# Second norm's root, inverse, shift and rows ahead of the score decays in each attention step, and the shared expert's weights split 512 columns at a time

## The reference, cut to what matters

```python
x = L0_attn_x
...
h = _layernorm(x, axis=-1) * (1 + ca) + sa
x = x + ga * _L0_attn_ref(h, slope_rate, W_qkvu, W_out)
h = _layernorm(x, axis=-1) * (1 + cb) + sb          # the second norm
x = x + gb * _L0_ffn_ref(h, wg, sh_gate, sh_up, sh_down, ex_gate, ex_up, ex_down)

def _layernorm(x, axis=-1, eps=1e-05):
    m = jnp.mean(x, axis=axis, keepdims=True)
    v = jnp.var(x, axis=axis, keepdims=True)
    return (x - m) / jnp.sqrt(v + eps)

# shared expert, over all tokens: silu(h @ sh_gate.T) * (h @ sh_up.T) @ sh_down.T
```

## Time and profile before

| what | us |
|---|---|
| median of 3 runs (lowest, highest) | 378.85 (378.01, 379.61) |
| the profiled execution, as timed | 375.64 |
| its span in the profile | 373.8 |
| attention steps 3 to 16 on TensorE | from 69.12 to 142.21 |
| feed-forward part | from 142.21 on |
| TensorE, VectorE, ScalarE, GpSimd busy, share of the span | 97%, 75%, 58%, 54% |

### The profile page before, as it was taken

The page is one execution under the profiler, slowest core; times in us unless marked ns, Lnnn a source line. Parts: engine busy times, 40 slices in busy tenths (PEclk is TensorE's granted clock), DMA queues, the critical chain, the costliest instruction groups (busy, mean ns, idle before and its releaser), DMA issues.

```text
span 373.8 us, 12932 instructions
## 1 busy us (share of the span) xinstructions
PE 362.9 (97%) x4978; PEld 315.0 (84%) x4983; DVE 280.2 (75%) x561; ACT 218.6 (58%) x453; POOL 200.8 (54%) x193
## 2 busy tenths in 40 slices
PE   8989998999999989999999999999999999999996
PEld 4546555778888769899999999999999999999995
DVE  7996388999899985579976987777777675555543
ACT  5688667677677755648276746555555634333222
POOL 2000003978778785311364687868767787674240
PEclk9999999999999999999999999999999999999999
DMA  8956031000197007999425465574685865665443
GB/s 265 375 63 60 2 134 37 2 4 30 32 353 184 31 31 265 330 336 271 88 92 108 104 110 104 95 118 88 104 109 91 100 101 103 100 114 77 70 58 113
DMA packets 53043, 45.35 MB, mean 121 GB/s; under 512 B 31524, under 2 KB 46996, under 8 KB 52856
## 3 DMA queue, kind: packets, MB, share of 16 engines
q1 hardware_dynamic: 43048, 32.09, 32.5%
q0 software_dynamic: 7488, 10.27, 18.2%
q10 hardware_dynamic: 2448, 2.18, 1.8%
HBM read 27.60 MB, written 10.49 MB: 102 GB/s over the span
## 4 chain that ended last, share of the span: by engine, by line
PE 72%; POOL 13%; DVE 7%; issue 5%; ACT 3%; ACTq 0%; POOLq 0%; DVEq 0%
PE ps L1630 37%; PE ps L1648 18%; PE ps L1413 7%; POOL tmp L554 3%; POOL tmp L558 2%; POOL tmp L575 2%; PE ps L1399 2%; POOL h2s L579 2%; POOL tmp L573 2%; POOL wx L563 2%; PE ps L1341 2%; DVE st L937 1%; PE ps L1533 1%; PE ps L1361 1%; DVE tmp L1254 1%
## 5 line engine op out<-in xcount | busy, mean ns | idle before, releaser
L1630 PE MATMUL ps<-tmp,wx 128*128 128x128 bf16 x1776 | 105.5, 219 | 0.0
L1630 PEld LDWEIGHTS ps<-tmp,wx 128*128 (+1 forms) x1776 | 102.3, 98 | 0.9 <-issue 0.2
L611 POOL DMA_INDIRECT out<-tmp,dk x39 | 72.0, 1846 | 38.0 <-SPq L515 32.5
L857 ACT ACTIVATE tmp<-tmp 128x512 bf16<-128x512 f32 x55 | 34.6, 629 | 80.8 <-PE ps L1648 61.6
L1648 PE MATMUL ps<-wx,tmp 128*128 (+1 forms) x660 | 80.7, 273 | 0.2 <-DVE tmp L1260 0.2
L1648 PEld LDWEIGHTS ps<-wx,tmp 128*128 128x128 bf16 x660 | 62.2, 98 | 6.9 <-DVE tmp L1260 0.5
L1254 DVE TENSOR_TENSOR tmp<-ps,tmp 128x512 f32<-128x512 f32 x55 | 37.9, 689 | 37.7 <-PE ps L1630 32.1
L1630 PE MATMUL ps<-w_hl,wx 128*128 128x128 bf16 x864 | 51.3, 219 | 0.9 <-ACT tmp L846 0.9
L606 POOL DMA_INDIRECT tmp<-h2rows,src_i x39 | 42.1, 1081 | 16.7 <-issue 10.8
L1630 PEld LDWEIGHTS ps<-w_hl,wx 128*128 (+1 forms) x864 | 49.6, 98 | 1.4 <-issue 1.0
L1260 DVE TENSOR_TENSOR tmp<-tmp 128x512 bf16<-128x512 f32 x55 | 38.3, 696 | 10.1 <-ACT tmp L857 9.9
(11 more groups left out here) (194 smaller groups left out, 555.2 us busy)
## 6 DMA issues: line engine op xcount, KB each, us to landing
wx<-in_wexp SPq DMA_DIRECT2D x26, 512.0 KB, 5.4
xres<-in_x SPq DMA_DIRECT2D x4, 512.0 KB, 6.6
h2rows<-h2s ACTq DMA_DIRECT2D x16, 128.0 KB, 3.4
out<-h2s SPq DMA_DIRECT2D x12, 128.0 KB, 2.1
h2s<-in_wmod SPq DMA_DIRECT2D x1, 1024.0 KB, 9.5
wx<-decay_rows SPq DMA_DIRECT2D x16, 64.0 KB
modr<-mod_rows SPq DMA_DIRECT2D x1, 1024.0 KB, 4.4
wx<-in_wqkvu SPq DMA_DIRECT2D x1, 768.0 KB, 6.8
```

The costliest lines, as they stand in the source:

```text
L611: e.indirect_dma_start(t["out"], bass.IndirectOffsetOnAxis(ap=dst_i[:, j:j + 1], axis=0), yb[(NA + j) % 2], None, compute_op=ALU.add).then ...
L857: e.activation(hs[p][:, 0:FF], hf[p], ACT.Copy).then_inc(s["inner_high"], 1)
L1630: ins = e.matmul(half(bank, m * P), weight(at_, weights(part, w) + k * FF + m * P, P), xT[f % NXT][:, (2 * a + k) * P:(2 * a + k + 1) * P] ...
```

## The change

VectorE: the decayed keys (L1075) now come behind the second norm's statistics (L1090). Behind them stand the inverse and the shift of the second norm (L1114 and L1116 before, L1098 and L1100 now), which stood behind the gated output; so they are ahead of the decay of the scores. ScalarE: the root (L746) comes ahead of the state's decay, and the normed rows (L774 before, L767 now) ahead of the squares and the turned rows. For the last tile (m = 15) VectorE makes the normed rows itself (L1105), and ScalarE at that place takes the silu of one column into a spare tile (L763). The shared weights are split in eight parts of 512 columns in steps 2, 3, 9, 10, 11, 12, 13, 14, where there were four of 1024 in steps 2, 9, 11, 13; the semaphore values that count parts are adapted.

```diff
-PARTS_AT, SCALED_AT = (2, 9, 11, 13), (0, 1, 2, 3)
+PARTS_AT, SCALED_AT = (2, 3, 9, 10, 11, 12, 13, 14), (0, 1, 2, 3)
...
@@ ScalarE, step_attention
                 if n and mine(n + 1):
                     mask_queries(n + 1)
+                if mine(m):
+                    wait(e, "ln2_moments", m + 1)
+                    e.activation(rs2[:, m % 2, 2:3], mv2[:, m % 2, 1:2], ACT.Sqrt, bias=epst[:, 0:1]).then_inc(s["ln2_root"], 1)
                 if mine(n, NSTATE) and n >= B:
...
-                if mine(m):
-                    wait(e, "ln2_moments", m + 1)
-                    e.activation(rs2[:, m % 2, 2:3], mv2[:, m % 2, 1:2], ACT.Sqrt, bias=epst[:, 0:1]).then_inc(s["ln2_root"], 1)
...
+                if m == NT - 1:
+
+                    e.activation(silu_back[:], epst[:, 0:1], ACT.Silu)
+                elif mine(m):
+                    wait(e, "ln2_shift", m + 1)
+                    wait(e, "h2_made", m - 1)
+                    e.activation(xn2[:, m % 2], xres[:, tile_of(m)[0]], ACT.Identity,
+                                 scale=rs2[:, m % 2, 3:4], bias=rs2[:, m % 2, 4:5]).then_inc(s["ln2_rows"], 1)
                 if mine(v):
                     wait(e, "values_added", v + 1)
...
-                if mine(m):
-                    wait(e, "ln2_shift", m + 1)
-                    wait(e, "h2_made", m - 1)
-                    e.activation(xn2[:, m % 2], xres[:, tile_of(m)[0]], ACT.Identity,
-                                 scale=rs2[:, m % 2, 3:4], bias=rs2[:, m % 2, 4:5]).then_inc(s["ln2_rows"], 1)
...
@@ VectorE, step_attention
-                if mine(n, NSTATE):
-                    wait(e, "k_turned", n + 1)
-                    wait(e, "kv_product", n - 1)
-                    e.tensor_tensor(kdec[:, n % 2, :], half(KT_BANK, 0, D), dk[:].rearrange("p h d -> p (h d)"), ALU.mult).then_inc(s["k_decayed"], 1)
...
                     e.bn_aggr(mv2[:, q, :], st2[:, q, :]).then_inc(s["ln2_moments"], 1)
+                if mine(n, NSTATE):
+                    wait(e, "k_turned", n + 1)
+                    wait(e, "kv_product", n - 1)
+                    e.tensor_tensor(kdec[:, n % 2, :], half(KT_BANK, 0, D), dk[:].rearrange("p h d -> p (h d)"), ALU.mult).then_inc(s["k_decayed"], 1)
...
+                if mine(m):
+                    wait(e, "ln2_root", m + 1)
+                    e.reciprocal(rs2[:, q, 3:4], rs2[:, q, 2:3]).then_inc(s["ln2_inverse"], 1)
+                    wait(e, "ln2_inverse", m + 1)
+                    e.scalar_tensor_tensor(out=rs2[:, q, 4:5], in0=mv2[:, q, 0:1], scalar=-1.0, in1=rs2[:, q, 3:4],
+                                           op0=ALU.mult, op1=ALU.mult).then_inc(s["ln2_shift"], 1)
+                if m == NT - 1:
+                    e.wait_ge(s["ln2_shift"], NT)
+                    e.wait_ge(s["h2_made"], m - 1)
+                    e.tensor_scalar(xn2[:, q], xres[:, tile], rs2[:, q, 3:4], rs2[:, q, 4:5], ALU.mult, ALU.add).then_inc(s["ln2_rows"], 1)
                 if mine(n) and n:
                     decay_scores(n)
```

More of the change, by code:

```diff
@@ L355, in weights, with shared_halves, down_halves, stage_halves @@
             return low * NPIECE * PIECE + part * PIECE
-        def shared_part(whole_, at_):
-            return whole_, wx[:, at_[0]:at_[0] + PIECE], wx[:, at_[1]:at_[1] + PIECE]
-        def both_halves(c):
-            return early_rows.rearrange("p (b c d) -> p b c d", b=B, d=D)[:, :, c:c + 2].rearrange("p b c d -> p b (c d)")
-        SHARED_PARTS = [shared_part(both_halves(NC - 4), [SHARED_AT + weights(2, a) for a in range(2)]),
-                        shared_part(both_halves(NC - 2), [SECOND_DOWN + a * PIECE for a in range(2)]),
-                        shared_part(early_stage[:, 0:PIECE], [SHARED_AT + weights(0, a) for a in range(2)]),
-                        shared_part(early_stage[:, PIECE:2 * PIECE], [SHARED_AT + weights(1, a) for a in range(2)])]
+        def shared_halves(whole_, at_):
+            return [(whole_[h], *(wx[:, at_[a] + h * PIECE // 2:at_[a] + (h + 1) * PIECE // 2] for a in range(2))) for h in range(2)]
+        def down_halves(c):
+            return [early_rows[:, (c + NC * b) * D:(c + 2 + NC * b) * D] for b in range(B)]
+        def stage_halves(q):
+            return [early_stage[:, q * PIECE + h * PIECE // 2:q * PIECE + (h + 1) * PIECE // 2] for h in range(2)]
+        SHARED_PARTS = [*shared_halves(down_halves(NC - 4), [SHARED_AT + weights(2, a) for a in range(2)]),
+                        *shared_halves(down_halves(NC - 2), [SECOND_DOWN + a * PIECE for a in range(2)]),
+                        *shared_halves(stage_halves(0), [SHARED_AT + weights(0, a) for a in range(2)]),
+                        *shared_halves(stage_halves(1), [SHARED_AT + weights(1, a) for a in range(2)])]
         SHARED_PARTS_AT = PARTS_AT
@@ L752, in step_attention @@
                     if h == NT - 8:
-                        e.wait_ge(s["shared_low"], 1)
+                        e.wait_ge(s["shared_low"], 2)
                     if h == NT - 4:
-                        e.wait_ge(s["shared_low"], 2)
+                        e.wait_ge(s["shared_low"], 4)
                     e.activation(h2s[:, tile_of(h)[0], 0:D], h2[:, h % 2], ACT.Copy).then_inc(s["h2_high"], 1)
+                if m == NT - 1:
[5 more added lines that the diff above has]
+                                 scale=rs2[:, m % 2, 3:4], bias=rs2[:, m % 2, 4:5]).then_inc(s["ln2_rows"], 1)
                 if mine(v):
@@ L786, in step_attention @@
                         e.wait_ge(s["shared_loaded"], 16 * 2)
-                    if n < SHARED_PARTS_AT[2]:
-                        high, whole_ = (a_.rearrange("p (b n) -> p b n", b=B) if len(a_.shape) == 2 else a_ for a_ in (high, whole_))
                     e.activation(high, whole_, ACT.Copy).then_inc(s["shared_high"], 1)
@@ L1090, in step_attention @@
                     e.bn_aggr(mv2[:, q, :], st2[:, q, :]).then_inc(s["ln2_moments"], 1)
+                if mine(n, NSTATE):
+                    wait(e, "k_turned", n + 1)
+                    wait(e, "kv_product", n - 1)
+                    e.tensor_tensor(kdec[:, n % 2, :], half(KT_BANK, 0, D), dk[:].rearrange("p h d -> p (h d)"), ALU.mult).then_inc(s["k_decayed"], 1)
+                if n == 0:
+                    queries_keys_low(3, (2,))
+                if mine(m):
[8 more added lines that the diff above has]
+                    e.tensor_scalar(xn2[:, q], xres[:, tile], rs2[:, q, 3:4], rs2[:, q, 4:5], ALU.mult, ALU.add).then_inc(s["ln2_rows"], 1)
                 if mine(n) and n:
@@ L1111, in step_attention @@
                     queries_keys_low(3, (3,))
-                if mine(m):
-                    wait(e, "ln2_root", m + 1)
-                    e.reciprocal(rs2[:, q, 3:4], rs2[:, q, 2:3]).then_inc(s["ln2_inverse"], 1)
-                    wait(e, "ln2_inverse", m + 1)
-                    e.scalar_tensor_tensor(out=rs2[:, q, 4:5], in0=mv2[:, q, 0:1], scalar=-1.0, in1=rs2[:, q, 3:4],
-                                           op0=ALU.mult, op1=ALU.mult).then_inc(s["ln2_shift"], 1)
                 if n - 1 in SHARED_PARTS_AT:
@@ L1121, in step_attention @@
                     e.wait_ge(s["shared_high"], x + 1)
-                    if x < 2:
-                        low, high = (a_.rearrange("p (b n) -> p b n", b=B) for a_ in (low, high))
                     e.tensor_tensor(low, whole_, high, ALU.subtract).then_inc(s["shared_low"], 1)
```

6 lines of the change are left out of this document (2 added, 4 removed).

## The result

| | us |
|---|---|
| changed kernel, median of 6 runs (lowest, highest) | 381.88 (381.42, 383.24) |
| kernel before, median of the 6 runs beside it | 378.51 (377.68, 379.61) |
| ratio, with its 95% interval | 1.0088 (1.0060 to 1.0116) |
| profiled executions, after and before | 381.42 and 375.64 |

The change costs 0.9% where no change was forecast; 381.88 lies outside the range of 375.5 to 380. The time is 1.88 above the range's upper end; the nearest rival is "VectorE stalls at the root" (379.95), yet the profile shows another mechanism than that rival's. The medians lie 3.37 apart and the profiled executions 5.78, since the profiled execution of before is 2.04 faster than the fastest of the six runs; so what the two profiles differ by is not all the change's.

A forecast was written before the change was run, and what follows sets the result against it. TensorE was taken to bound full attention steps (5.22 us), VectorE those in and just behind weights parts. Terms 0.2 - 0.3 - 0.35 + 0.55 - 1.05 = -0.95, say -1.0, took 378.85 to 377.85 us; range 375.5 to 380.

The forecast's parts named there:

- VectorE stalls at the root: Rival: ScalarE reaches the second norm's root later than counted, lengthening each split step on VectorE; 379.95 us, chance 0.13.
- The halves: VectorE, steps with a 512-column low half: each half costs 0.61 us start to start, making the step 5.45.
- The root's wait: VectorE, each step: the decay stands behind ScalarE's second-norm root, leaving 0.11 us of wait per step.
- Start, +0.2: Attention steps 3 to 6: later first decay and two steps of 5.45 start step 6 0.2 us later.
- Steps 10 to 13, -0.3: Attention steps 10 to 13: VectorE decays 5.45 apart put S(14) at 127.35; gain 0.3 us, the start's 0.2 taken off.
- 14 and 15, -0.35: Steps 14 and 15: waits for GpSimd go, VectorE takes their place; stretch 10.35 against 10.73, gain 0.35 us.
- Step 16, +0.55: Step 16: TensorE's logits wait for ScalarE's turned rows; values of tile 15 to first gate 4.55 against 4.01 us.
- Steps 17 to 19, -1.05: Steps 17 to 19: silu's table load moves behind the last root, so tile 2's gate starts 1.05 us sooner.
- Loads, at nothing with +1.6 as the bound: SyncE's loads of experts 3 to 7 start some 0.6 us later; costed at nothing, up to +1.6 without slack.

The follow-up runs named there:

- rows_back: The changed kernel with ScalarE's normed rows back where the kernel before has them, for all tiles but the last; ratio to the kernel before 1.0035.
- silu_only: The kernel before with only the last tile's normed rows made by VectorE and silu's tables loaded early; ratio to the kernel before 0.9998.
- changed_again: The changed kernel run once more, unaltered, as reference for variants on the same chip; ratio to the kernel before 1.0051.
- turn8: The changed kernel with the rows of shared tile 8 turned by TensorE in place of a DMA transpose; ratio to the kernel before 1.0091.
- norm_only: The changed kernel with the shared weights in four parts of 1024 columns in place of the eight halves; ratio to the kernel before 1.0061.
- halves_silu_t8: The changed kernel with the second norm's order put back as before and tile 8 turned on TensorE; ratio to the kernel before 0.9946.

## Why the prediction was wrong, point by point

- **The halves** are the step that failed. I took 0.61 from start to start from a row far from the attention and let all eight cost that. Without the norm's order they do (5.32 against 4.73 is 0.59). In steps 10 to 13 of the changed kernel one costs 1.11 to 1.13 (111.65 to 112.76 in step 10). In the changed kernel, the excess over 0.68 up to the decay of tile 15 is 0.35, 0, 0.51, 0.52, 0.52, 0.51 and 0.28, in all 2.69 us. That decay was forecast at 135.4 and came at 138.09. That this is 2.69 too is partly luck, since counted from the decay of tile 2 it is 2.90. But a step of 5.97 less its 0.52 is the 5.45 of the forecast, and of the 3.05 us between the forecast's -0.95 and the stretch's +2.10 the halves' excess is 2.69. I had the row that warned of it, the 784 ns mean of L554 against the 0.73 of a single one, and used it as a duration. The mechanism, two VectorE inputs in SBUF beside a GpSimd product, was in no rival.
- **The root's wait**, 0.11 per step: right in size by rows_back, and 0.31 in step 10, where 0.11 and 0.27 had been summed. It is not what most of the time went to.
- **Start, +0.2:** step 6 came 0.45 later, 0.66 counted from the decay of tile 2. The first half took 1.03.
- **Steps 10 to 13, -0.3,** and **14 and 15, -0.35:** scores of tile 14 at 129.14 (forecast 127.35), values of tile 15 at 141.43 (137.7). TensorE's waits for GpSimd's shift did go, as said; VectorE took their place by 2.7 us more than I summed, and the logits waited 0.68 for ScalarE's turned rows in step 14 (L1546 at 133.99), which the sum has in step 16 alone.
- **Step 16, +0.55:** the wait for the turned rows is there (0.34 ahead of L1546 at 144.54), but from the values to the first gate it is 3.66 us, not 4.55, and 4.01 before. The lag had already been paid on the values. From the decay of tile 15 to the first gate it is 7.00, forecast 6.85.
- **Steps 17 to 19, -1.05:** the table load (1.28 at 151.17) moved, the gate of tile 2 starts 0.22 behind the turn, and from first gate to gate of tile 2 it is 8.67 us against 9.45. That is -0.78; the mechanism right, the size 0.27 short. The silu of one column follows the load at once (152.46), so a load cost 1.28 here and no more. VectorE's rows of tile 15 took 0.78 where silu_only has 0.41; whether that makes the difference was not tried.
- **Loads, at nothing with +1.6 as the bound:** in the profile of after, 1.35 us. In changed_again, whose loads took 27.11 us, nothing. The bound held, the value of nothing did not follow from 0.30 of idle time in an execution whose turn had 9.0 us of lead.
- **VectorE stalls at the root** came nearest to the time, 1.93 too low, by the wrong cause: no inverse waited longer than 0.31 in a step with keys. Its own sign, "decays over 5.7 apart", appeared, so that sign did not tell the causes apart; the duration of the low half did.
- The stretch accounts for 2.1 to 2.3 us of the 3.4 between the medians (1.9 on the chip of changed_again). The rest may be the wait for the turn. It stays open, since turn8, whose profile is free of that wait, has the same ratio.

## What to carry to other kernels

When work on GpSimd is brought earlier, ask what VectorE runs at its new time: in the attention steps of these traces an instruction of VectorE with two SBUF inputs and a GpSimd product took turns, and whoever issued second waited for the other's end. In a pipeline whose engines keep one rhythm, a small lead decides which engine pays, and then it pays in every step (in rows_back 0.03 to 0.04 us of lead put the price on GpSimd in steps 11 to 13, in the changed kernel a lag of 0.07 to 0.09 put it on VectorE in steps 10 to 13); keep such instructions in the idle time of the other, or let the engine with slack come second. A small move of an order should be tested apart from a change of sizes beside it: here one part gained 0.3% and the other took back four times that.

## What the runs showed of the hardware

- A GpSimd product of 256 columns lasts 0.67 to 0.73 us alone. Second to a 512-column VectorE instruction with two SBUF inputs it lasted up to 1.27 (changed_again, step 4), second to one of 1024 up to 1.79 (norm_only, step 3). In all these meetings the one that came second lasted longer by what was left of the first when it was issued, to the end of its row, less 0.12 to 0.16 us. VectorE's part came second 29 times in the attention steps of the fourteen traces, with an excess of 0.04 to 0.52, and there the 0.12 to 0.16 were 0.12 to 0.14, for either width. VectorE's decay of 128x2048, with one input in PSUM, lasted 2.27 to 2.29 in all kernels, whatever GpSimd did beside it.
- Small instructions pay too. Two of the router's (a comparison and a product, 128x96, two SBUF inputs, 0.26 each before) took 0.58 and 0.74 in the changed kernel, beside GpSimd's low half of the rows (L583 at 146.75) and its scale (L558 at 147.47). The shift of one column (0.16 alone), begun while a GpSimd product ran, lasted to within 0.03 us of the end of that product's row, 0.19 to 0.62 in all, in the kernel before too. One case does not fit the order of the rows: the shift of 0.71 in changed_again (above) starts 0.02 ahead of GpSimd's L577 (71.73, 0.67) and yet waited that one out. The router's rows:

```profile
146.95 0.58 DVE L1154 TENSOR_TENSOR w_hl<-logit,w_hl 128x96 f32<-128x96 f32 x1
147.57 0.74 DVE L1155 TENSOR_TENSOR w_hl<-w_hl,kept 128x96 f32<-128x96 f32 x1
```

- Even an instruction with one SBUF input did: the 128x256 rows with a scale and a shift per row took 0.41 us in silu_only, 0.78 here, begun 0.04 after GpSimd's L583. That is 0.37 longer, where 0.63 less 0.13 would be 0.50; why it is less, no run shows:

```profile
151.27 0.78 DVE L1105 TENSOR_SCALAR tmp<-xres,rs 128x256 f32<-128x256 f32 x1
```

```profile
151.23 0.67 POOL L583 TENSOR_TENSOR h2s<-tmp,h2s 128x256 bf16<-128x256 f32 x1 [2.22 <-ACT h2s L760]
```

- The same 18 weight loads took 27.1 (changed_again) to 31.7 us (halves_silu_t8) in different runs.
